# Attention in a four-layer block: where the heads' outputs are divided by their row sums

## The reference, cut to what matters

```
xn = rms_norm(x, gamma)
qkv = xn @ w_qkv                        # q, k, v: 16 heads of 64
sim = einsum('bhid,bhjd->bhij', q * scale, k)
attn = softmax(sim, axis=-1)            # each row divided by its sum
out = einsum('bhij,bhjd->bhid', attn, v)
return out.reshape(b, n, 1024) @ w_out
```

## Time and profile before

| | |
|---|---|
| median of three runs | 2229.23 us (2208.46, 2229.23, 2532.37) |
| the profiled execution | 2211.21 us, span 2208.7 us |
| mean granted TensorE clock | 0.944 of full speed |
| busy: PE, DVE, ACT, POOL | 92%, 84%, 69%, 64% of the span |
| attention | from about 640 to 2162 us of the span |

### The profile page before, as it was taken

One profiled execution on the slowest core, in us unless ns is written; L12 is line 12 of the kernel. 1 busy time (PEld: TensorE's weight loads), 2 busy tenths in 40 slices (PEclk: granted clock), 3 DMA queues, 4 the chain that ended last, 5 costly groups with the idle time before them and its releaser, 6 DMA issues. The chain is left out here.

```text
span 2208.7 us, 30463 instructions
## 1 busy us (share of the span) xinstructions
PE 2034.0 (92%) x8352; PEld 1451.9 (66%) x8352; DVE 1846.7 (84%) x1997; ACT 1523.8 (69%) x1877; POOL 1414.5 (64%) x660
## 2 busy tenths in 40 slices
PE   6999648999868999999999999999999999999887
PEld 4777427777645766766666676676667667666554
DVE  5888776887567899898889889889989988999785
ACT  4666435665326878777778778778778777787764
POOL 1000010000206899899999889989989998999882
PEclk7999758998778999999999999999999999999998
DMA  3210002110050213032131312303213031230000
GB/s 113 70 45 26 0 0 59 47 47 15 0 118 1 55 34 68 19 67 62 27 68 21 67 42 47 68 14 72 51 38 68 16 72 31 55 68 17 6 1 19
DMA packets 77271, 94.71 MB, mean 43 GB/s; under 512 B 31755, under 2 KB 35211, under 8 KB 76870
## 3 DMA queue, kind: packets, MB, share of 16 engines
q1 hardware_dynamic: 77142, 93.04, 18.5%
HBM read 41.11 MB, written 1.42 MB: 19 GB/s over the span
## 5 line engine op out<-in xcount | busy, mean ns | idle before, releaser
L490 POOL TENSOR_TENSOR p_l<-p_raw,p_h 128x1024 fp32r<-128x1024 f32 x512 | 1241.6, 2461 | 166.0 <-ACT p_h L1085 154.1
L1082 ACT ACTIVATE p_raw<-ps 128x1024 f32<-128x1024 f32 x512 | 566.7, 1107 | 257.4 <-PE ps L718 254.6
L1401 DVE TENSOR_REDUCE m_part<-ps 128x1 f32<-128x1024 f32 x480 | 584.3, 1217 | 143.9 <-PE ps L695 143.3
L1085 ACT ACTIVATE p_h<-ps 128x1024 fp32r<-128x1024 f32 x512 | 524.4, 1024 | 0.0
L717 PE MATMUL ps<-qa,ka 128*128 128x512 f32 x1024 | 447.4, 437 | 15.7 <-issue 13.7
L718 PE MATMUL ps<-qb,kb 65*128 65x512 f32 x1024 | 410.1, 400 | 0.0
L732 PE MATMUL ps<-p_h,v_hl 128*128 128x512 f32 x1024 | 404.2, 395 | 1.5 <-POOL p_l L490 1.3
L1395 DVE TENSOR_REDUCE l_sum<-p_raw 128x128 f32<-128x1280 f32 x256 | 377.0, 1476 | 0.4
L695 PE MATMUL ps<-ka,qa 128*128 128x512 f32 x960 | 315.1, 409 | 12.3 <-DVE m_part L1401 12.3
L735 PE MATMUL ps<-p_l,v_hl 128*64 128x512 f32 x1024 | 321.5, 395 | 0.0
L1381 DVE TENSOR_REDUCE p_raw<-p_raw 128x128 f32<-128x1024 f32 x256 | 309.0, 1208 | 13.0 <-ACT p_raw L1082 13.0
(11 more groups left out here) (185 smaller groups left out, 2681.4 us busy)
## 6 DMA issues: line engine op xcount, KB each, us to landing
big<-g_scratch SPq DMA_DIRECT2D x64, 256.0 KB, 3.2
xnp<-r_scratch SPq DMA_DIRECT2D x59, 256.0 KB, 3.9
qa<-qk_hi SPq DMA_DIRECT2D x112, 128.0 KB, 2.3
ka<-qk_hi SPq DMA_DIRECT2D x56, 128.0 KB, 2.3
kb<-qk_hi SPq DMA_DIRECT2D x56, 128.0 KB, 2.4
ka<-xnp SPq DMA_DIRECT2D x28, 128.0 KB, 2.4
qb<-xnp SPq DMA_DIRECT2D x28, 128.0 KB, 2.4
ka<-qk_low SPq DMA_DIRECT2D x28, 128.0 KB, 2.7
```

What stands on the lines that cost most here:

```text
L490: nc.gpsimd.tensor_tensor(p_l[:, g % 4, :, :], slots(g), p_h[:, g % 4, :, :].bitcast(fp32), ALU.subtract).then_inc(pl_done, 1)
L1082: af(slots(g), s_t, ACT.Exp).then_inc(raw_done, 1)
L1085: af(p_h[:, g % 4, :, :], s_t, ACT.Exp).then_inc(ph_done, 1)
L1401: nc.vector.tensor_reduce(m_part[:, it, half:half + 1], ps[:, 4:6, :].rearrange("p b n -> p (b n)"), AX.X, ALU.max).then_inc(s_max, 1)
```

## The change

POOL's `scale` goes, with its semaphore `o_scaled`. `project_out` waits for `o_done` (the copy by ACT) in its place and projects the unscaled output. `add_out` on DVE is now two instructions: a multiplication of the projected bank by `r_bc`, in place in PSUM, and, after a wait for its end (`out_scaled`), the addition to `x` as before. Its first instruction also waits for `r_loaded`. `invert` waits for the addition before it (`out_add`), since `r_bc` is one buffer that the next load overwrites. In the last head `project_out` of the late chunk moves from group 5 to 3 and its `add_out` from group 6 to 4.

```diff
-END_TURN, END_LATE_OUT, END_LATE_ADD = 3, 5, 6
+END_TURN, END_LATE_OUT, END_LATE_ADD = 3, 3, 4
...
-            def scale(head, c):
-
-                k = chunk_of(head, c)
-                pool.wait_ge(r_loaded, 16 * (k + 1))
-                pool.wait_ge(o_done, k + 1)
-                nc.gpsimd.tensor_tensor(o_raw[:, c % 2, :], o_raw[:, c % 2, :], r_bc, ALU.mult).then_inc(o_scaled, 1)
-
             def window(pair, par, project):
...
-                        if g == SCALE_GROUP:
-                            scaled = before(head, c, 2)
-                            if exists(scaled[0]) and not (last and c > 0):
-                                scale(*scaled)
...
-                pe.wait_ge(o_scaled, k + 1)
+                pe.wait_ge(o_done, k + 1)
                 mm(ps[:, bank, :], w_o[par][:, :], o_raw[:, c % 2, :], start=True, stop=True).then_inc(out_ps, 1)
...
                 if not (isinstance(k, int) and k == 0):
-                    dve.wait_ge(o_scaled, k)
+                    dve.wait_ge(out_add, k)
                 nc.vector.reciprocal(r_col[:, c % 2, :], l_col[:, c % 2, :]).then_inc(r_ready, 1)
 
             def add_out(head, c, bank):
-                dve.wait_ge(out_ps, chunk_of(head, c) + 1)
+                k = chunk_of(head, c)
+                dve.wait_ge(out_ps, k + 1)
+                dve.wait_ge(r_loaded, 16 * (k + 1))
+                tt(ps[:, bank, :], ps[:, bank, :], r_bc, ALU.mult).then_inc(out_scaled, 1)
+                dve.wait_ge(out_scaled, k + 1)
                 stt(x[:, chunk(c)], ps[:, bank, :], 1.0 / C, x[:, chunk(c)], ALU.mult, ALU.add).then_inc(out_add, 1)
 
             def end_invert(i, bank):
...
                 if i == 0:
-                    dve.wait_ge(o_scaled, NC * (HEADS - 1) - 1)
+                    dve.wait_ge(out_add, NC * (HEADS - 1) - 1)
```

More of the change, by code:

```diff
@@ L45 @@
 V_SPLIT = ((0, 3), (1, 0))
-SCALE_GROUP = 3
 COPY_GROUP = 2
@@ L215, in macaron_kernel @@
         l_stored, l_loaded = sem("l_stored"), sem("l_loaded")
-        r_ready, r_stored, r_loaded, o_scaled = sem("r_ready"), sem("r_stored"), sem("r_loaded"), sem("o_scaled")
+        r_ready, r_stored, r_loaded, out_scaled = sem("r_ready"), sem("r_stored"), sem("r_loaded"), sem("out_scaled")
         out_ps, out_add = sem("out_ps"), sem("out_add")
@@ L506, in low_v_weights @@
                 nc.gpsimd.tensor_tensor(wv_hl[:, 1, :], wv_raw[:, :], wv_hl[:, 0, :].bitcast(fp32), ALU.subtract).then_inc(vw_lo, 1)
-            def scale(head, c):
-                k = chunk_of(head, c)
-                pool.wait_ge(r_loaded, 16 * (k + 1))
-                pool.wait_ge(o_done, k + 1)
-                nc.gpsimd.tensor_tensor(o_raw[:, c % 2, :], o_raw[:, c % 2, :], r_bc, ALU.mult).then_inc(o_scaled, 1)
             def window(pair, par, project):
                 head = 2 * pair + par
-                last = isinstance(head, int) and head == HEADS - 1
                 for c in range(NC):
```

## The result

The changed kernel takes 2265.64 us (median of four, 2258.04 to 2271.45) against 2226.44 us (median of four, 2208.46 to 2532.37). The ratio, 1.0202 with a 95% interval of 1.013 to 1.0273, leaves out the run of 2532.37 us, a slow one. So the changed kernel is slower; whether by more than 2%, these runs do not tell. The profiled execution takes 2265.9 us, 54.7 more than the profiled one of before; the forecast was 38 more.

The account below looks back on a forecast made before the run. PE sets the pace and DVE's maxima hold it up; POOL follows. From the profiled 2211.2 us, plus 40.6 in the loop and the pairs around it, less 3.0 at the end: 2248.8 us, range 2222 to 2273.

Parts of the forecast that it names:

- The bound and the follower: In the loop PE sets the pace, held by DVE about twice a chunk; POOL only follows, so relieving it gains nothing.
- The place and the passing on: In group 0, DVE's added time reaches PE whole at a pair with 0.06 us to spare: 43 x 0.85 = 36.6 us.
- the multiplication and POOL shut each other out: Rival: the new multiplication and POOL exclude each other, +2 us or more at 59 places, 2330 us; 2%.
- The price: DVE's cost per addition followed by `invert`: 0.85 us, made of 0.72 for the multiplication and 0.13 for the held reciprocal.
- 0.13 more: The reciprocal, waiting for the addition's end, starts 0.72 us behind the addition's start in place of 0.59.
- The bound of 0.97: Upper bound in us per addition followed by `invert`, if the write to PSUM costs 0.12 more.
- Group 7: Additions in group 7 of chunk 3: 0.57 us pass in seven first heads, 4.0 us; nothing in second heads.
- Swallows 0.72 whole: Second heads' group 7: PE stands 2.87 us at the loop's branch, DVE waits 4.73 us, so the multiplication costs nothing.
- the clock as a rival: PE's longer stalls lower its clock; if in one chunk of two, +50 us, 2299 us; 4%.
- The end: Last head: the long reciprocal and multiplication L1433 come earlier; a gain of 1.2 to about 5 us, taken as 3.
- Without the scale that run ends some 1.2 us sooner: Last head: POOL's run of four L490, after which L1433 ended, ends earlier without POOL's scale step.
- the lower of the two gains named: Last head: 1.2 us if L1433 again lets POOL's run end, against about 5 if it gets in earlier.

Follow-up runs that it names:

- e5_nopool: The kernel before without POOL's scale step and nothing in its place (last head's long reciprocal waits for `r_loaded`): 2216.25 us beside 2218.18, ratio 0.9993.
- e1_both: The changed kernel with POOL's scale step put back and DVE's multiplication in PSUM and all waits kept: ratio 1.0224, loop stage 1362.54 us against 1362.37.
- e2_nomult: The changed kernel without the multiplication, its waits kept: 2222.97 us, ratio 1.0031 to the kernel before, chunks 0.24 us over before.
- e3_later: The changed kernel with the small reciprocal moved from group 0 to group 1 in chunks 1 to 3: 2253.66 us, ratio 1.0160 to the kernel before.

## Why the prediction was right, and where its sizes were off

**The bound and the follower: right.** The waits said that nobody waits for POOL. e5_nopool (0.00 us a chunk) and e1_both (0.2 us in 1362) show it from both sides.

**The place and the passing on: right.** The 43 chunks with an addition in group 0 are longer by 0.97 us, where the one looked at has 0.95 more on DVE ahead of the maximum and 0.06 between the maximum and PE's pair. DVE's idle time elsewhere in the chunk took none of it. Nor did the multiplication and POOL shut each other out: 0.69 us in all 59.

**The price, mis-sized: 0.85 us was forecast, 0.97 measured**, 5.1 us over 43. The multiplication was right (0.72). The term that failed was the reciprocal held behind the addition, "0.13 more": e2_nomult has 0.24 and e3_later 0.25. I took the pitch of a dependent pair from the earlier trace rows, where one instruction waits for one semaphore. In the loop the reciprocal waits for two, and a register update stands between; there the pitch is 0.80, and the maximum behind the reciprocal comes 0.11 later in place of 0.09. No run tells which of the two differences makes the 0.08. The bound of 0.97 was for another reason (a dear write to PSUM) and held by luck: the multiplication into PSUM took 0.689 us, where the addition into SBUF took 0.680. By the Trainium skill's rule (VectorE: DVE Perf Modes, The DRAIN you can't avoid) the semaphores would have been free. The runs disagree: moving one instruction out from behind a wait, with the same work, gave back 0.25 us a chunk.

**Group 7: 4.0 us forecast in the first heads, 2.9 measured; none forecast in the second heads, 7.9 measured.** "Swallows 0.72 whole" failed by some 0.25 to 0.5 us a crossing. The larger part, some 5 us, is the clock behind PE's stall at the loop's end. I had the clock as a rival for new stalls inside the chunks. There it stayed at 1.00; it was the old stall, now 0.4 us longer, behind which it fell more often. Over all ten traces some 5 of the 7.3 us at the loop's ends go with the change, so the sum had put at nothing a term of about 5 us, and about 2 are chance.

**The end: -3 us was forecast, +4.1 measured, and 0.9 ahead of it.** "Without the scale that run ends some 1.2 us sooner" came out to the tenth: counted from the 58th projection, the long reciprocal comes 2.3 us earlier, the scaling 2.9, the end of POOL's run 1.2, and the first chunk's projection 1.2, the lower of the two gains named. Of the rest, 1.6 us lie behind the attention. What the step left out is that four of the five scalings are drawn anew whenever anything ahead of them moves: the last went from 2.96 to 7.83 us. Which way they fall is luck, as far as these traces go: the last stage took 139.5 to 147.0 us in the seven kernels that have them. I had read the row of 5.00 us as one delay to be shortened and not as one of four, 2.7 to 8.3 us each, that could all be taken out.

**The sum** was 38 us for 54.7 in the profiled pair: 12 of the difference in the loop (5 price, 5 clock, 2 crossings, less 1 in group 7, and rounding), 8 at the end, of which 1.6 behind the attention, and -2 ahead of the attention, which is spread. On medians it was 2249 forecast and 2265.6 measured, within the range. Part of that gap is the choice of 2211.2 us as the start: three later sessions have the kernel before at 2218 to 2219 us (medians of 11 to 19 runs), so the change costs some 47 us, if the sessions compare, where 38 were forecast. "Same" had 68% and "slower by over 2%" 30%, and a ratio of 1.0202 confirms neither. That 2265.6 lies in the range is in part luck: its upper end held 18 us for the level of the median, and the clock at the loop's ends and the last head's scalings used them up.

## What to carry to other kernels

Of engines that are all near 90% busy, ask who is waited for, and where. One that is full for 20 us and that nobody waits for can be relieved of work without gain (here 57 steps of 1.3 us in the loop stage); one that idles 10% of the time can have none to spare between two steps of a single buffer. There an added instruction is paid in full, and a wait of an engine for its own last instruction too, so put an independent instruction between. A mechanism can be wrong in the loop and right at the end: look for the stage where the receiving engine has room and the other is waited for.

## What the runs showed of the hardware

VectorE multiplies 512 fp32 columns in place in PSUM by an SBUF operand in 0.69 us (686 to 692 ns in 59), beside a busy GpSimd too; its addition from PSUM into SBUF took 0.68. With both inputs in SBUF the multiplication took 0.69 us with GpSimd idle and 0.85 to 8.28 us with GpSimd busy. The Trainium skill (SBUF — State Buffer, Who interferes with whom) calls the port pair that the two engines share an exclusive lock. The rows agree that it isn't shared: the delayed ones end 0.55 us behind the end of a GpSimd instruction, and where another GpSimd instruction follows at once, that one is longer by some 0.5 us. But the order of arrival doesn't decide: GpSimd's instructions are 2.4 to 2.5 us each, and VectorE waited up to 8.28 - 0.69 = 7.6 us, more than three of them. It was passed over more than once, and the profile books that time as busy.
